# A four-layer graph network on one core: layer 2's scores from stacked high and low parts, layer 3's attention in one bank, centred weights, new orders

## The chip, the cores and the metric

The kernel runs on one core of a Trainium2 chip. Its time is the device time of one execution in microseconds; where several runs are given, their median. Four compute engines work side by side: TensorE (PE in the profile, with its weight loads as PEld), VectorE (DVE), ScalarE (ACT) and GpSimd (POOL); SyncE (SP) issues the DMAs.

## The reference, cut to what matters

128 graphs of 64 nodes with 256 features pass through four layers, each added to its input and normalised over the features.

```python
x = _layernorm(x + _L0_gnn_ref(x, adj, ...), axis=-1)      # hypergraph convolution, twice
x = _layernorm(x + _L1_gnn_ref(x, adj, nodemask, ...), axis=-1)
x = _layernorm(x + _L2_gnn_ref(x, adj, adj, ...), axis=-1)
x = _layernorm(x + _L3_gnn_ref(x, adj, ...), axis=-1)
# layer 2: 8 heads of 32
scores = jnp.einsum('bhqd,bhkd->bhqk', q, k) * SCALE * mask      # mask = adj + adj
ctx = jnp.einsum('bhqk,bhkd->bhqd', jax.nn.softmax(scores, axis=-1), v)
# layer 3
gate = jax.nn.sigmoid(deg * Wd[:, 0] + bd); xg = x * gate
QK = jax.nn.sigmoid(xg @ Wqk.T + bqk)
scores = jnp.einsum('bnd,bmd->bnm', QK, QK) / math.sqrt(D) * adj
attn = scores / (jnp.sum(scores, axis=-1, keepdims=True) + 1e-06)
out = jax.nn.relu(jnp.einsum('bnm,bmd->bnd', attn, xg) @ Wl.T + bl + xg @ Wr.T)
```

## The kernel before

**Tiles and numbers.** A group is four graphs, that is two tiles of 128 rows, each of two graphs (b = 0, 1). There are 32 groups. Every product is taken with operands split into a high and a low part of 16 bits, and three matmuls stand for one (high by high, high by low, low by high; `mm3`, L479 to L483). The splits are made by ScalarE (high part, a cast) and VectorE or GpSimd (low part, a subtraction).

**Steps and streams.** The work of a group is cut into six streams, `stream0` to `stream5` on each engine, which lie in six successive steps: in step s, stream k works on group s - k. Layer 0 is in streams 0 and 1, layer 1 in streams 1 and 2, layer 2 in streams 2 to 4, layer 3 in streams 4 and 5. So 32 + 5 steps are run; those from 6 on are a loop over pairs of steps, the first six and the last five are written out.

**Orders.** On each engine a list written out by hand or by a planner (`ORDER_PE`, `ORDER_ACT`, `ORDER_DVE`, `ORDER_POOL`; `HEAD_...` and `TAIL_...` for the steps outside the loop) tells which stream's next piece comes next. An engine takes its pieces strictly in this order and waits at each for its semaphores.

**SyncE** has one queue in a fixed order (`step`, L436): `place_k` (L386), the loads of the next groups for conv, residual, layer 2, gate and layer 3, those of layer 1, `place_v`, then `store`. Each of them waits on SyncE where it has to, and all behind it waits too.

**Layer 2 scores.** Queries `qh`, `ql` and keys `kst` have the features of four heads on 128 rows. `place_k` copies the keys to a block-diagonal `Kbd` with four copies, zeros elsewhere, so that one matmul of 256 columns gives four heads; 12 such matmuls make the scores of a tile (L677).

**Layer 3 attention** (stream 5) lives in bank bG: projections, sigmoid through tanh, scores of a whole tile of two graphs (128 x 128, masked by a block-diagonal adjacency `atG`), the product with Wr (`o2`, with the bias `blb` added by VectorE, L1237), row sums by matmul (L749), then the mix scaled by the reciprocal of the sums on VectorE (L1252), ReLU on ScalarE (L937), and the residual added on GpSimd (`preG`, L1399).

**Normalisations** B, C, F and G: VectorE's statistics (`stats`, L1021), GpSimd's `rstd` (L1285: add epsilon, power -0.5, two products `nb`), ScalarE's `norm` (L780).

Of the kernel before, what the change touches and what calls it, by code (L numbers as in the profile page):

```python
# [50 lines left out]
HEAD_DVE = [[0, 0, 0, 0, 0, 0, 0, 0, 0, 0, 6, 6, 6, 0, 6, 6, 6, 0, 6, 0, 6, 0, 0], [0, 0, 0, 0, 0, 0, 1, 0, 0, 0, 0, 1, 1, 1, 0, 6, 1, 1, 0, 6, 1, 0, 1, 0, 0], [0, 0, 0, 2, 0, 2, 0, 0, 1, 2, 0, 0, 0, 2, 0, 1, 1, 1, 0, 2, 2, 2, 6, 1, 6, 0, 2, 1, 2, 0, 1, 0, 0, 1], [0, 0, 6, 6, 0, 0, 1, 2, 0, 2, 0, 0, 0, 0, 3, 6, 1, 2, 0, 2, 1, 1, 6, 0, 2, 2, 2, 3, 3, 6, 3, 3, 3, 1, 2, 0, 1, 3, 2, 1, 0, 3, 0, 0, 1, 6], [4, 0, 0, 0, 0, 0, 2, 0, 2, 4, 1, 0, 0, 0, 4, 4, 4, 0, 2, 3, 4, 0, 2, 1, 1, 3, 1, 4, 2, 2, 2, 4, 4, 3, 3, 3, 1, 0, 3, 2, 1, 3, 1, 2, 0, 4, 0, 1, 3, 0], [0, 0, 2, 0, 4, 4, 2, 0, 3, 0, 0, 1, 0, 4, 4, 0, 0, 3, 4, 2, 2, 0, 1, 3, 1, 3, 4, 1, 0, 2, 2, 5, 2, 5, 4, 4, 3, 4, 5, 3, 1, 5, 0, 5, 2, 1, 5, 5, 1, 3, 5, 0, 5, 1, 3, 0, 0, 2, 4]]
HEAD_POOL = [[6, 6, 0, 0, 0, 0, 0, 0, 0, 0, 0, 0], [0, 0, 0, 1, 1, 0, 6, 1, 1, 1, 6, 1, 6, 6, 0, 0, 0, 0, 0, 0], [0, 0, 0, 1, 1, 0, 1, 1, 1, 6, 2, 2, 6, 2, 0, 6, 0, 0, 1, 0, 0, 0], [0, 1, 0, 0, 1, 0, 1, 1, 1, 3, 2, 2, 2, 3, 3, 0, 0, 0, 1, 0, 0, 0], [0, 0, 0, 0, 1, 4, 1, 3, 1, 1, 1, 1, 2, 2, 4, 2, 4, 4, 0, 3, 0, 3, 4, 0, 0, 0, 0], [3, 0, 0, 0, 1, 1, 4, 0, 1, 3, 1, 1, 2, 2, 2, 0, 4, 3, 5, 4, 0, 4, 0, 1, 5, 4, 5, 5, 5, 0, 0, 0]]
TAIL_PE = [[1, 2, 3, 5, 4, 2, 4, 2, 1, 4, 5, 2, 3, 5, 4, 5, 1, 3, 5, 5, 3, 1, 2, 2, 4, 1, 3, 3], [5, 3, 2, 4, 5, 2, 4, 3, 2, 5, 4, 2, 3, 4, 5, 3, 5, 5, 2, 2, 3, 3, 4], [3, 5, 4, 4, 5, 3, 5, 4, 3, 5, 4, 5, 3, 5, 3, 3, 4], [4, 4, 5, 4, 5, 4, 5, 5, 5, 5, 4], [5, 5, 5, 5, 5, 5]]
TAIL_ACT = [[1, 3, 2, 4, 5, 5, 4, 5, 3, 5, 1, 1, 4, 4, 2, 5, 4, 2, 3, 1, 4, 3, 2, 5, 3], [5, 3, 5, 5, 2, 4, 3, 4, 4, 5, 4, 2, 3, 2, 5, 4, 3, 2, 4, 3, 5], [3, 5, 5, 4, 5, 3, 4, 5, 4, 4, 3, 5, 4, 3, 3, 4, 5], [4, 5, 4, 5, 4, 5, 4, 5, 4, 5, 4, 5], [5, 5, 5, 5, 5, 5]]
# [1387 lines left out]
```

## Time and profile before

| | us |
|---|---|
| runs | 997.31, 999.5, 1002.46; median 999.5 |
| the profiled execution | 999.49, of which the span is 997.7 |
| busy of the span: PE, DVE, POOL, ACT | 928.4, 836.6, 746.0, 702.5 |
| mean granted clock of TensorE | 0.977 of full speed |

The span is from the first to the last instruction of the trace. Busy time of an engine is the sum of its instructions' time without overlap. In an order of time ("timeline") each line has the start, the duration of one piece, the engine, the line of the kernel, what is written and what is read, and how many; brackets at the end hold the idle time ahead of it and what ended it. Matmuls overlap, so the cost of a string of them is read from start to start, not from their durations.

### The profile page before, as it was taken

What the parts mean: (1) busy time and instruction counts of PE and PEld (TensorE: products, weight loads), DVE (VectorE), ACT (ScalarE), POOL (GpSimd) and SP (SyncE); (2) the same over time, 40 slices, a digit from 0 to 9 for tenths busy, and PEclk for the clock granted to TensorE, in tenths of its full rate; (3) what the DMA queues carried; (4) which work ended last, traced back from release to release, by engine and by line L of the source; (5) the groups of instructions that cost most, each with busy time, mean ns of one, the idle gap of its engine ahead of it and who ended that gap; (6) DMA issues with size and microseconds to landing.
All of it is one profiled execution on the core that took longest, in us unless ns stands there. A gap on an engine that the chain in (4) does not pass through costs nothing. (4 is left out here: it accounts for less than half of the span.)

```text
span 997.7 us, 32479 instructions
## 1 busy us (share of the span) xinstructions
PE 928.4 (93%) x11228; PEld 812.0 (81%) x11228; DVE 836.6 (84%) x2503; ACT 702.5 (70%) x1516; POOL 746.0 (75%) x1169
## 2 busy tenths in 40 slices
PE   4687899999999999999999999999999999999854
PEld 3566788888888888888888888888888888887642
DVE  4467888898998999899988899899989898988752
ACT  3445667777777777877787777787787777776552
POOL 2655768878878888888888888888888888876551
PEclk9779999999999999999999999999999999999995
DMA  7102221222222222222222222222222222212200
GB/s 238 40 9 60 58 68 50 56 54 61 71 71 71 56 68 53 58 61 61 71 71 71 59 66 56 56 59 65 68 71 71 63 63 67 54 37 52 52 20 21
DMA packets 110231, 61.80 MB, mean 62 GB/s; under 512 B 57072, under 2 KB 105840, under 8 KB 110192
## 3 DMA queue, kind: packets, MB, share of 16 engines
q1 hardware_dynamic: 110192, 61.30, 23.4%
q8 instruction: 22, 0.36, 0.1%
q14 instruction: 17, 0.14, 0.0%
HBM read 35.83 MB, written 8.39 MB: 44 GB/s over the span
## 5 line engine op out<-in xcount | busy, mean ns | idle before, releaser
L784 ACT ACTIVATE late<-preG,nbG,rsG 128x256 f32<-128x256 f32 x64 | 34.9, 592 | 63.1 <-POOL nbG L1295 63.1
L481 PE MATMUL bank<-z1h,W 128*128 128x256 f16 x256 | 72.0, 281 | 3.8 <-DVE z1l L951 3.6
L482 PE MATMUL bank<-z1l,W 128*128 128x256 f16 x256 | 72.0, 281 | 0.0
L483 PE MATMUL bank<-z1h,W 128*128 128x256 f16 x256 | 72.0, 281 | 0.0
L1374 POOL TENSOR_TENSOR late<-late,Smx 128x512 f32<-128x512 f32 x64 | 67.5, 1055 | 4.7 <-DVE Smx L1182 4.7
L481 PE MATMUL bank<-W,rFh 128*128 128x256 f16 x256 | 70.7, 276 | 0.0
L483 PE MATMUL bank<-W,rFl 128*128 128x256 f16 x256 | 70.7, 276 | 0.0
L482 PE MATMUL bank<-W,rFh 128*128 128x256 f16 x256 | 70.7, 276 | 0.0
L1300 POOL TENSOR_TENSOR gp<-late,bdb 128x512 f32<-128x512 f32 x32 | 40.7, 1271 | 32.7 <-ACT late L897 32.7
L813 ACT ACTIVATE r<-bank,b1c 128x256 f32<-128x256 f32 x128 | 52.6, 463 | 16.7 <-PE bank L483 16.7
L1283 POOL TENSOR_TENSOR y0l<-y,y0h 128x512 f16<-128x512 f32 x32 | 37.2, 1163 | 31.6 <-ACT y0h L766 31.6
L1325 POOL TENSOR_TENSOR rsq<-rsq 128x512 f32<-128x512 f32 x32 | 54.6, 1705 | 4.3 <-ACT rsq L821 2.2
L766 ACT ACTIVATE z1h<-bank 128x512 f16<-128x512 f32 x32 | 19.1, 598 | 50.2 <-PE bank L483 50.2
L1283 POOL TENSOR_TENSOR rFl<-r,rFh 128x512 f16<-128x512 f32 x32 | 37.3, 1165 | 18.9 <-ACT rFh L766 18.9
L784 ACT ACTIVATE x<-preB,nbB,rsB 128x256 f32<-128x256 f32 x64 | 34.9, 593 | 22.0 <-POOL nbB L1295 22.0
L677 PE MATMUL bank<-Kbd,qh 128*64 128x256 f16 x512 | 47.1, 279 | 1.9 <-DMA Kbd<-kst 1.7
L951 DVE SCALAR_TENSOR_TENSOR PTl<-bank,PTh 128x512 f16<-128x512 f32 x64 | 43.6, 681 | 2.6 <-ACT PTh L766 2.6
L1399 POOL TENSOR_TENSOR preG<-o3r,late 128x512 f32<-128x512 f32 x32 | 40.8, 1274 | 6.4 <-ACT o3r L937 5.6
L1177 DVE TENSOR_TENSOR late<-bank,acD 128x512 f32<-128x512 f32 x64 | 43.5, 680 | 2.2 <-PE bank L677 2.1
L481 PE MATMUL bank<-Wv,x2Fh 128*128 128x128 f16 x256 | 44.8, 220 | 0.0
L483 PE MATMUL bank<-Wv,x2Fl 128*128 128x128 f16 x256 | 44.5, 219 | 0.0
L482 PE MATMUL bank<-Wv,x2Fh 128*128 128x128 f16 x256 | 44.5, 219 | 0.0
(286 smaller groups left out, 4519.0 us busy)
## 6 DMA issues: line engine op xcount, KB each, us to landing
Vbd<-vst SPq DMA_DIRECT2D x128, 66.0 KB, 2.1
xin<-x SPq DMA_DIRECT2D x32, 256.0 KB, 2.7
xres<-x SPq DMA_DIRECT2D x32, 256.0 KB, 2.9
Kbd<-kst SPq DMA_DIRECT2D x128, 64.0 KB, 2.0
out<-late SPq DMA_DIRECT2D x32, 256.0 KB, 2.2
mrow<-mask SPq DMA_DIRECT2D x32, 128.0 KB, 3.1
atA<-adj_t SPq DMA_DIRECT2D x64, 32.0 KB, 2.3
aC<-adj SPq DMA_DIRECT2D x64, 32.0 KB, 2.1
```

Source lines behind the costliest of these rows:

```text
L481: pe.matmul(o, sh, mh, start=start, stop=False, skip_group_check=True)
L482: pe.matmul(o, sh, ml, start=False, stop=False, skip_group_check=True)
L483: return pe.matmul(o, sl, mh, start=False, stop=stop, skip_group_check=True)
L677: m = pe.matmul(o[64 * b:64 * b + 64, c * 256:(c + 1) * 256], qq[:, c, tok], Kbd[:, :, hl, c, tok], start=(i == 0), stop=(i == 2), skip_gr ...
L784: m = act.activation(dst[:, t], pre[k][:, t], ACT.Identity, bias=nb[k][:, t:t + 1], scale=rs[k][:, t:t + 1])
L813: m = act.activation(r[:, 2 * i + c], (bA, bB)[i][:, c * TOK:(c + 1) * TOK], ACT.Relu, bias=b1c[:, 2 * i + c:2 * i + c + 1], scale=1.0 / WS)
L951: return dve.scalar_tensor_tensor(out=dst, in0=src, scalar=scale, in1=hi, op0=ALU.mult, op1=ALU.subtract)
L1177: dve.tensor_tensor(Sm[:, t], (bD0, bD1)[t][:].rearrange("p (h k) -> p h k", h=HEADS), acD[:, at.par, t:t + 1].broadcast_to([P, HEADS, NOD ...
L1283: return pool.tensor_tensor(dst, a, b, ALU.subtract)
L1325: pool.tensor_tensor(rsq[:, 0:2], rsq[:, 0:2], rsq[:, 2:4], ALU.add).then_inc(ev("sq_sum"), 1)
L1374: pool.tensor_tensor(Ssb[:, t], Sm[:, t], Smx[:, t:t + 1].rearrange("p t h -> p h t").broadcast_to([P, HEADS, NODES]), ALU.subtract).then_ ...
L1399: pool.tensor_tensor(pre["G"][:], o3r[:], x3[:, at.par], ALU.add).then_inc(ev("preG"), 1)
```

## The change

It has five parts.

1. Layer 2's scores. Queries are kept as `qst` with both parts, like `kst`. Both are written to DRAM (`park_q`, `park_k`), and read back by head: 32 rows for a head, with three stacks of 32 rows, `Qs` with high, high, low and `Ks` with high, low, high. One matmul over 96 rows then makes the three products of a head, 64 columns at a time; 16 make a tile's scores. `Kbd` and its clearing go. In SyncE's queue `park_k` takes the first place, `fetch_k` comes behind the loads for conv and residual, `load_layer3` goes behind `place_v`, then `park_q`, `store`, `fetch_q`.
2. Layer 3's attention. Scores are made for each graph alone, 64 x 64 in half of a bank, and masked with their row sums in one operation. They are divided by the sums before the mix (`SAs`, on GpSimd), turned once on TensorE, and split. The bias enters by a matmul of 512 columns, the product with Wr and the mix are added onto it in bG, and VectorE applies ReLU and residual in one operation.
3. Wv1, Wo and bo are centred over the features at the start, so that C and F need no mean: their `rstd` has two operations, and `norm` only a scale. Factors go into the epsilon operations.
4. The second half of `rFl` goes from VectorE to GpSimd; `rsc` comes straight from the power.
5. All orders are new.

```diff
-ORDER_PE = [3, 2, 1, 5, 0, 2, 4, 4, 3, 2, 5, 1, 0, 2, 0, 4, 3, 5, 0, 0, 3, 1, 5, 4, 5, 1, 3, 2, 5, 3, 1, 0, 2, 0, 4]
+ORDER_PE = [1, 2, 3, 5, 3, 0, 4, 4, 2, 1, 2, 0, 5, 4, 0, 2, 5, 3, 3, 0, 1, 0, 4, 5, 1, 2, 5, 3, 5, 2, 3, 1, 0, 0, 4]
-ORDER_ACT = [0, 5, 2, 3, 5, 1, 3, 0, 4, 5, 0, 0, 4, 4, 1, 4, 0, 5, 0, 0, 1, 0, 0, 2, 0, 3, 1, 3, 2, 5, 4, 3, 2, 4, 5]
+ORDER_ACT = [3, 1, 5, 5, 0, 2, 0, 4, 0, 3, 5, 4, 0, 4, 4, 1, 1, 0, 0, 0, 2, 5, 3, 0, 0, 2, 0, 1, 3, 4, 3, 2, 4, 5]
-ORDER_DVE = [0, 2, 0, 0, 2, 0, 0, 0, 0, 4, 1, 3, 4, 0, 4, 0, 2, 4, 4, 2, 5, 1, 0, 1, 3, 1, 5, 0, 2, 2, 2, 5, 3, 4, 3, 3, 3, 1, 5, 4, 0, 4, 5, 4, 5, 1, 5, 2, 1, 0, 3, 0, 5, 5, 1, 0, 3, 2, 4]
+ORDER_DVE = [0, 0, 0, 1, 0, 2, 0, 2, 0, 4, 3, 0, 4, 0, 0, 4, 4, 4, 1, 2, 5, 0, 1, 2, 3, 1, 5, 0, 4, 2, 5, 2, 5, 3, 2, 3, 5, 1, 3, 4, 3, 5, 4, 4, 2, 1, 5, 1, 5, 3, 0, 5, 0, 2, 0, 3, 1, 4]
...
+            def park(name, dram, at):
+
+                sp.dma_start(dram[at.par].rearrange("l p k -> p l k"),
+                             (qst if name == "q" else kst)[:].rearrange("p l c k -> p l (c k)")
+                             ).then_inc(ev(name + "_parked"), 16)
+
+            def fetch(name, dram, dst, parts, at):
+
+                sp.wait_ge(ev(name + "_parked"), at.chain(16, 16)).then_inc(ev("sp_held"), 1)
+                for r, hl in enumerate(parts):
+                    sp.dma_start(dst[32 * r:32 * r + 32].rearrange("p a c k -> p a (c k)"),
+                                 dram[at.par][hl].rearrange("(a p) k -> p a k", p=32)
+                                 ).then_inc(ev(name + "_stacked"), 16)
+
+            def park_q(at):
+                sp.wait_ge(ev("q_lo"), at.n()).then_inc(ev("sp_held"), 1)
+                park("q", q_by_head, at)
+
+            def fetch_q(at):
+                fetch("q", q_by_head, Qs[:, at.par], (0, 0, 1), at)
+
+            def park_k(at):
                 sp.wait_ge(ev("k_lo"), at.n()).then_inc(ev("sp_held"), 1)
+                park("k", k_by_head, at)
+
+            def fetch_k(at):
                 if at.earlier(1):
                     sp.wait_ge(ev("scores"), at.tile(1, -1)).then_inc(ev("sp_held"), 1)
-                for h in range(4):
-                    sp.dma_start(Kbd[32 * h:32 * h + 32, h], kst[32 * h:32 * h + 32]
-                                 ).then_inc(ev(f"k_bd{at.par}"), 16)
+                fetch("k", k_by_head, Ks, (0, 1, 0), at)
...
-                    place_k(at)
-
+                    park_k(at)
                 for k, load in enumerate(loads):
                     at = At(k, j, s + 1)
-                    if load and there(at):
+                    if load and k != 5 and there(at):
                         load(at)
+                    at = At(3, j, s)
+                    if k == 1 and there(at):
+                        fetch_k(at)
...
+                at = At(5, j, s + 1)
+                if there(at):
+                    load_layer3(at)
+                at = At(2, j, s)
+                if there(at):
+                    park_q(at)
                 at = At(5, j, s)
                 if there(at):
                     store(at)
+                at = At(2, j, s)
+                if there(at):
+                    fetch_q(at)
...
-                pe.wait_ge(ev(f"k_bd{at.par}"), at.dma(4))
+                pe.wait_ge(ev("q_stacked"), at.chain(48, 48))
+                pe.wait_ge(ev("k_stacked"), at.chain(48, 48))
...
-                        for i, (qq, hl) in enumerate(((qh, 0), (qh, 1), (ql, 0))):
+                        for a in range(4):
                             for b in range(2):
                                 tok = slice(t * P + 64 * b, t * P + 64 * b + 64)
-                                m = pe.matmul(o[64 * b:64 * b + 64, c * 256:(c + 1) * 256], qq[:, c, tok],
-                                              Kbd[:, :, hl, c, tok], start=(i == 0), stop=(i == 2),
+                                h = 4 * c + a
+                                m = pe.matmul(o[64 * b:64 * b + 64, h * NODES:(h + 1) * NODES],
+                                              Qs[:, at.par, a, c, tok], Ks[:, a, c, tok], start=True, stop=True,
                                               skip_group_check=True)
...
+                pe.wait_ge(ev("attn_scaled"), at.n())
+                pe.transpose(bG[:, D + P:2 * D], SAs[:].rearrange("p b k -> p (b k)"), ident[:]
+                             ).then_inc(ev("attn_turned"), 1)
...
+                pe.matmul(bG[:].rearrange("p (t d) -> p t d", t=TILES), ones16[:, 0:1].broadcast_to([P, P]),
+                          blr[:].rearrange("p (o d) -> p o d", o=1).broadcast_to([P, TILES, D]), start=True, stop=False,
+                          skip_group_check=True)
+                for t in range(TILES):
+                    m = project_tm(bG[:, t * D:(t + 1) * D], xgFh, xgFl, Wr, t, onto=True)
                 m.then_inc(ev("o2_raw"), 1)
...
+                    for i, (sa, y) in enumerate(((SAh, y3h), (SAh, y3l), (SAl, y3h))):
+                        for b in range(2):
+                            rows = slice(64 * b, 64 * b + 64)
+                            m = pe.matmul(bG[rows, t * D:(t + 1) * D], sa[rows, t], y[rows, t], start=False,
+                                          stop=(i == 2), skip_group_check=True)
                 m.then_inc(ev("o1"), 1)
...
+                for b in range(2):
+                    m = dve.tensor_tensor_reduce(SA[:, b], bG[:, D + b * NODES:D + (b + 1) * NODES], atG[:, at.par, b],
+                                                 1.0, 0.0, ALU.mult, ALU.add, bG[:, b:b + 1])
+                m.then_inc(ev("attn"), 1)
...
+                dve.scalar_tensor_tensor(out=pre["G"][:].rearrange("p t k -> p (t k)"), in0=bG[:], scalar=0.0,
+                                         in1=x3[:, at.par].rearrange("p t k -> p (t k)"), op0=ALU.max, op1=ALU.add
+                                         ).then_inc(ev("preG"), 1)
...
-                dve.wait_ge(ev("rF_hi"), at.tile(1))
-                dve.tensor_tensor(rFl[:, 2:4], r[:, 2:4], rFh[:, 2:4], ALU.subtract).then_inc(ev("rF_lo1"), 1)
-                yield
...
+                pool.wait_ge(ev("rF_hi"), at.tile(1))
+                sub(rFl[:, 2:4], r[:, 2:4], rFh[:, 2:4]).then_inc(ev("rF_lo1"), 1)
+                yield
...
-                pool.wait_ge(ev("attn_hi"), at.n())
-                sub(SAl[:].rearrange("p t k -> p (t k)"), SA[:], SAh[:].rearrange("p t k -> p (t k)")
-                    ).then_inc(ev("attn_lo"), 1)
-                yield
-                pool.wait_ge(ev("o3_relu"), at.n())
-                if at.earlier(1):
-                    pool.wait_ge(ev("xG"), at.n(-1))
-                pool.tensor_tensor(pre["G"][:], o3r[:], x3[:, at.par], ALU.add).then_inc(ev("preG"), 1)
+                pool.wait_ge(ev("row_scale"), at.chain(2, 2))
+                pool.tensor_tensor(SAs[:], SA[:], srec[:].rearrange("p (t o) -> p t o", o=1).broadcast_to(
+                    [P, TILES, NODES]), ALU.mult).then_inc(ev("attn_scaled"), 1)
```

## Rows read from the trace of the kernel before

**Rows 1.** The page, part 1: busy us, share of the span, instructions of each engine.

```profile
PE 928.4 (93%) x11228; PEld 812.0 (81%) x11228; DVE 836.6 (84%) x2503; ACT 702.5 (70%) x1516; POOL 746.0 (75%) x1169
```

**Rows 2.** Windows, one step: length, busy PE, PEld, DVE, ACT, POOL; clock, DMA share, GB/s.

```profile
525.33:553.18 27.85, 27.85 (x352) 25.02 (x350) 25.21 (x78) 21.63 (x47) 22.96 (x36) 1.00 0.24 64
```

**Rows 3.** Timeline of SyncE: start us, duration us, what, count.

```profile
194.74 2.49 SPq L392 DMA_DIRECT2D Kbd<-kst  x4
...
529.34 0.42 SPq L407 DMA_DIRECT2D out<-late  x1
...
532.34 2.48 SPq L392 DMA_DIRECT2D Kbd<-kst  x4
...
535.09 0.40 SPq L345 DMA_DIRECT2D xin<-x  x1
...
538.30 0.37 SPq L369 DMA_DIRECT2D acD<-adj  x1
...
840.07 2.48 SPq L392 DMA_DIRECT2D Kbd<-kst  x4
```

**Rows 4.** Timeline of TensorE, one step: start us, duration us, what, count.

```profile
524.84 0.66 PE L506 MATMUL bank<-ident,late 128*128 128x128 f32 x4
...
525.33 0.27 PE L481 MATMUL bank<-x2Fh,Wk 128*128 128x256 f16 x1
...
529.91 0.26 PE L701 MATMUL bank<-Vbd,PTh 128*64 128x66 f16 x4
...
530.80 0.23 PE L481 MATMUL bank<-Wv,x2Fh 128*128 128x128 f16 x1
...
537.04 0.41 PE L677 MATMUL bank<-Kbd,qh 128*64 128x256 f16 x4
...
537.82 0.23 PE L481 MATMUL bank<-Qh 128*128 128x128 f16 x1
...
538.50 0.27 PE L481 MATMUL bank<-z1h,W 128*128 128x256 f16 x1
...
547.39 0.27 PE L481 MATMUL bank<-y3h,SAh 128*128 128x256 f16 x1
...
548.04 0.60 PE L688 MATMUL bank<-ident,E 128*128 128x128 f32 x4
...
553.18 0.27 PE L481 MATMUL bank<-x2Fh,Wk 128*128 128x256 f16 x1
```

**Rows 5.** Timelines of ScalarE and VectorE, the beginning of the same step.

```profile
525.53 0.60 ACT L766 ACTIVATE xgFh<-bank 128x512 f16<-128x512 f32 x1 [0.98 <-PE bank L506]
...
526.18 0.68 DVE L951 SCALAR_TENSOR_TENSOR xgFl<-bank,xgFh 128x512 f16<-128x512 f32 x1
...
526.77 0.32 DVE L1035 TENSOR_SCALAR HT<-atA 128x256 f16<-128x256 f32 x1
...
529.87 0.16 DVE L1060 TENSOR_SCALAR Dbg<-bank 128x2 f32<-128x2 f32 x1 [0.72 <-PE bank L557]
...
531.24 0.88 DVE L957 SCALAR_TENSOR_TENSOR kst<-bank,bkc,kst 128x256 f16<-128x256 f32 x2 [0.23 <-ACT kst L869]
```

**Rows 6.** Instruction groups by form: busy us, mean ns, idle before.

```profile
L1237 DVE SCALAR_TENSOR_TENSOR late<-bank,blb 128x512 f32<-128x512 f32 x32 | 21.8, 680 | 3.6 <-PE bank L483 3.6
...
L1295 POOL TENSOR_SCALAR nbF<-mvF,rsF 128x1 f32<-128x1 f32 x64 | 16.0, 267 | 6.2 <-POOL rsF L1291 6.0
...
L1399 POOL TENSOR_TENSOR preG<-o3r,late 128x512 f32<-128x512 f32 x32 | 40.8, 1274 | 6.4 <-ACT o3r L937 5.6
```

**Rows 7.** Chain of work that ended last, tail: start us, us, what.

```profile
941.94 2.05 DMA Kbd<-kst
944.03 0.85 PE bank L677 x12
```

**Rows 8.** DMA issues: KB each, median us from issue to landing.

```profile
out<-late SPq DMA_DIRECT2D x32, 256.0 KB, 2.2
...
acD<-adj SPq DMA_DIRECT2D x32, 64.0 KB, 2.4
```

More of the change, by code:

```diff
@@ L129, in build @@
         x3, x4 = [v.rearrange("p a (t d) -> p a t d", t=TILES) for v in (x3, x4)]
-        cx, gw, xg, o2, o3 = [late[1][:, i] for i in range(5)]
+        cx, gw, xg = [late[1][:, i] for i in range(3)]
         Sm, Ssb = [v.rearrange("p t (h k) -> p t h k", h=HEADS) for v in (Sm, Ssb)]
@@ L864, in stream3 @@
             def stream3(at):
+                if at.earlier(1):
+                    act.wait_ge(ev("k_parked"), at.chain(16, 16, -1))
                 act.wait_ge(ev("k"), at.n())
-                if at.earlier(1):
-                    act.wait_ge(ev(f"k_bd{1 - at.par}"), at.before().dma(4))
                 for c in range(2):
@@ L977, in part, with centre @@
                     low(W[:, 1], split_from[name], W[:, 0], WS).then_inc(ev("unstaged"), 1)
+                def centre(rows, sums, done):
+                    dve.tensor_reduce(wmean[:, sums], rows, AX.X, ALU.add).then_inc(ev("centring"), 1)
+                    dve.wait_ge(ev("centring"), done + 1)
+                    dve.tensor_scalar(wmean[:, sums], wmean[:, sums], -1.0 / D, None, ALU.mult
+                                      ).then_inc(ev("centring"), 1)
+                    dve.wait_ge(ev("centring"), done + 2)
+                    for i in range(rows.shape[1]):
+                        k = sums.start + i
+                        m = dve.tensor_scalar(rows[:, i], rows[:, i], wmean[:, k:k + 1], None, ALU.add)
+                    m.then_inc(ev("centring"), 1)
                 dve.wait_ge(ev("w2_in"), 64)
@@ L1009, in set_up @@
                 m.then_inc(ev("setup"), 1)
+                dve.tensor_scalar(blr[:], blf[:], WS, None, ALU.mult).then_inc(ev("bl_row"), 1)
+                dve.wait_ge(ev("bl_row"), 1)
+                low(blr[32:33], blf[32:33], blr[32:33], WS).then_inc(ev("bl_row"), 1)
                 yield
-                for i in range(2, 7):
+                part(2)
+                yield
+                dve.wait_ge(ev("second_in"), 32)
+                centre(stages["Wv1"], slice(0, 2), 0)
+                yield
+                part(3)
+                yield
+                dve.wait_ge(ev("rest_in"), arrival("Wo")[1])
+                centre(stages["Wo"], slice(2, 4), 3)
+                yield
+                centre(bob[:].rearrange("p (o d) -> p o d", o=1), slice(4, 5), 6)
+                yield
+                for i in range(4, 7):
                     part(i)
@@ L1246, in stream5 @@
                 yield
[L1247 to L1254 removed]
+                dve.wait_ge(ev("attn_hi"), at.n())
@@ L1270, in set_up @@
             def set_up():
-                for h in range(4):
-                    pool.memset(Kbd[:, h], 0.0).then_inc(ev("ident"), 1)
-                    yield
                 for par in range(2):
```

199 lines of the change are left out of this document (99 added, 100 removed).

## The prediction

> **What bounds the kernel now.** I read the page's busy line first: TensorE is busy 93% of the span, VectorE 84% [rows 1]. The window of one whole step in the middle shows more: TensorE busy all of its 27.85 us, VectorE 25.2, at the full granted clock [rows 2]. Then SyncE's order of time: the first copy of layer 2's keys is issued at 194.74 and at 840.07, 23 steps apart, so a step costs 28.06 us on average [rows 3]; 26 steps run like that, and the first six and last five are partly filled. TensorE's own order of time gives the places inside a step, which I count from the end of the turn of `xg` (525.33, the last item of `ORDER_PE`, in both orders): scores of tile 0 at 11.71, next step at 27.85 [rows 4]. Nothing but TensorE's work sets the time in these steps. Last, what lies ahead of the scores on other engines: ScalarE and VectorE take `xgF` first, then a string of short operations, then the low half of `kst` [rows 5], then SyncE's four issues [rows 3].
>
> **The change, part by part.** All of it per step, in us.
>
> TensorE. (a) Scores: the two tiles took 12 matmuls of 256 columns each, 0.78 a tile (537.04 to 537.82). Now 16 matmuls of 64 columns a tile. The nearest row is the context product, 48 matmuls of 66 columns in 0.89 (529.91 to 530.80), 0.0185 each [rows 4]: 0.30, or 0.37 with the entry into the pattern. Two tiles save 0.82. (b) Layer 3 scores: 0.68 (537.82 to 538.50) becomes 24 matmuls of 64 columns, 0.44: saves 0.24. (c) One more turn of 128 columns: a quarter of 0.49 (524.84 to 525.33), 0.12; the bias row, 512 columns at twice 0.108 (six of 256 columns in 0.65, 547.39 to 548.04), 0.22. (d) `o1`, six matmuls of 256 columns over 128 rows, becomes twelve over 64 rows. If the two halves of a pair run beside each other, as the 64-column pairs of the context product do, it stays 0.65, plus 0.08 for leaving the pattern; if they follow one another it is 1.30. I take the first. Row sums and their waits are counted at nothing. Sum: -0.82 -0.24 +0.12 +0.22 +0.08 = -0.64, between -0.9 and 0.0. TensorE alone would make the step 27.4.
>
> VectorE loses `o2` (0.68) and half of `rFl`, and gains a 128-column low part; GpSimd loses `preG` (1.27) and the two `nb` of C and of F (0.27 each), and gains `rFl`'s other half; ScalarE loses the ReLU [rows 6]. None of these ends a step today [rows 2], so this is worth nothing in the 26 steps.
>
> SyncE and DMA. Four copies of keys go; a write of K to DRAM, a wait, three reads, and the same for Q come: eight for four. Q has a whole step. K has not, and this is the part that I cost in full.
> - VectorE's step begins 1.44 after the turn of `xg`, since `xgFh` and `xgFl` come first (525.33 to 526.77 [rows 5]); the new orders end with the same three items.
> - From there to the low part of `kst` it was 4.47, of which 0.72 was a wait for TensorE and 0.23 a wait for ScalarE [rows 5]. The new order has the same operations ahead of it but one of 0.08: 3.44. The keys are now projected third on TensorE, done by 2.8, and ScalarE's part is over by 3.8 if it is as long as VectorE's; no wait. So it starts at 4.9 and ends at 5.77 (0.88 long). SyncE issues 0.22 later, as now (532.12 to 532.34 [rows 3]): 5.97.
> - `park_k` takes one issue, 0.42 with 0.27 behind it, as a store does [rows 3]. Then, in the same queue and ahead of `fetch_k`, come the loads of x, of two blocks of the adjacency and of the residual: 3.21 (535.09 to 538.30 [rows 3]). The write lands in 2.2, like the store [rows 8], so within that time. `fetch_k` starts at 5.97+0.69+3.21+0.1 = 9.97.
> - Its third issue starts 1.24 later (0.62 each, 2.48 for four [rows 3]) and lands in 2.05 (copy within SBUF [rows 7]) to 2.4 (load [rows 8]); I take 2.2, nearest to a store or load of this size. Keys are there at 13.4, between 12.9 and 14.2 (the ends: three issues at 0.5 and the short landing; issues at 0.8, as the blocks with short rows take, and the long one).
> - TensorE's items ahead of scores are the same set as before plus layer 3's scores, 11.71+0.44 = 12.15. It waits 1.25.
> - Behind the wait lies all of its queue: what took 16.14 (537.04 to 553.18) less 0.68, 0.82 and plus 0.42 is 15.06. A step is 13.4+15.06 = 28.46, against 28.06: +0.40, between 0 and +1.2. Over 26 steps +10.
>
> The Trainium skill (DMA: Bandwidth & Descriptors, "Anatomy of one DMA") says that most of a transfer's fixed 2 us is the receipt of its write, heaviest where the target is HBM. The rows here show 2.2 for the store to DRAM and 2.05 within SBUF, so the heavier target costs 0.2; by either figure the write is covered by the loads queued behind it.
>
> Why the wait isn't repaid: VectorE's start is tied to TensorE's last item, so what TensorE waits moves the next chain by as much.
>
> Edges. In the last steps no loads stand between, so K costs 0.4+2.2+1.2+2.2 = 6.0 from the low part where now it is 1.9+2.05 = 3.95 [rows 3, 7]: +2 at each of two to three places. The chain through layer 3 loses a GpSimd addition (1.27), `o2` (0.68), and 0.54 for each pair of `nb` of C and F [rows 6], and the ReLU, some of it in two places: about -6 in the last steps. The head loses GpSimd's clearing of `Kbd`, which nothing waits for, and gains centring on VectorE. I put 0 on the edges, between -5 and +6. Profiled execution 999.49 (span 997.7), the median 999.5: the same. Sum: 1010.
>
> **Rivals.** One: the keys arrive in time and TensorE stays dense. For it: the copies now have 0.8 in hand (issued at 7.01 after the origin, landed by about 10.9, used at 11.71), and an error of 1.2 in a chain of ten terms is possible. Then a step is 27.4, 26 times -0.66 is -17, with the shorter layer 3 chain -3: 979. Against it: the ready time would have to be 12.15, and even the short ends of all DMA terms give 12.9.
>
> Two: `o1`'s halves follow one another. The row at issue is 547.39, six matmuls that use all 128 rows; no row shows a 64-row one. 0.65 more per step, behind the scores and so on the path: +17, that is 1027; slower from the point where the pair overlaps by less than nine tenths. The Trainium skill (TensorEngine Tiling (Array Packing), "Gotcha 1: PSUM Pressure" and "Key Properties") states that row tiles can't use one PSUM bank at the same time and that a change of tiling mode drains the engine, and both halves of `o1` write the bank bG. No row here shows it; by this rule the sum would be this rival's.
>
> Three: SyncE is late at `park_k`. Ahead of it stand the store and `fetch_q`: the store was issued at 529.34, 4.0 after the origin [rows 3]; GpSimd's string for G is a bit shorter and earlier, so I take 3.1, an estimate, then 0.7 and three issues of 0.62: free at 5.7, 0.3 before it is needed. If the stacked reads take 0.8 an issue, this slips by 0.3 and `fetch_k` by 0.4, and with a store as late as today by 0.9 more: about +1 a step, 1036.
>
> That the change doesn't do what it says (K no longer on the path at all) is rival one.
>
> **How the numbers follow.** Forecast 1010 (own range 1000 to 1022), chance 0.46; rival one 979, 0.26; two 1027, 0.14; three 1036, 0.14. The range leaves out one in ten on each side: 977 to 1035. Half a per cent, 5 us, is about what a measurement of this kernel can tell from no change. Faster by more (under 994.5): rival one and a little of the forecast, 0.28. Within: a quarter of the forecast and the slow edge of rival one, 0.16. Slower: 0.56. Step by step the weakest term is the landing of 128 KB reads with 32 rows each, which the trace of before doesn't hold.
>
> **What would show it.** TensorE's line idle once per step ahead of the first score matmul, about 1.2 us, released by a DMA into `Ks`; the rest of the step dense; a step of 28.4 between issues; score tiles of 0.37 apart; `o1` in 0.65 to 0.73; VectorE's share lower. The issues from `park_k` to the first `fetch_k` 4 us apart. If scores start within 0.1 of the item ahead, the chain was mis-sized and rival one holds; if the idle time is released by Q's reads, it is rival three; a second idle place in the step would be one that I have not costed.

## The result, and the profile after

The changed kernel takes 1083.3 us (median of 4 runs, 1079.0 to 1088.6); the kernel before, beside it, 998.4 us. The ratio is 1.085, with a 95% interval of 1.078 to 1.093: slower by 85 us, where the prediction had 1010. The profiled execution has a span of 1086.7 us.

The page of the changed kernel: busy time of each engine, the clock line of the 40 slices, two lines of the parts on the chain and on DMA issues, and the group of layer 2's scores.

```profile
PE 949.9 (87%) x11996; PEld 825.9 (76%) x11996; DVE 792.9 (73%) x2548; ACT 676.9 (62%) x1484; POOL 686.0 (63%) x1005
...
PEclk9798899989999999899999999998999999999997
...
PE 42%; DVE 15%; SPq 13%; DMA 11%; issue 10%; POOL 4%; ACT 4%; POOLq 0%; ACTq 0%; DVEq 0%
...
L719 PE MATMUL bank<-Ks,Qs 96*64 96x64 f16 x1024 | 29.3, 219 | 72.4 <-DMA Ks<-k_by_head 72.2
...
Ks<-k_by_head SPq DMA_DIRECT2D x96, 128.0 KB, 3.0
```

Every engine but TensorE is busy for less time than before [rows 1], so no engine became the bound. TensorE's busy time *rose* by 21.5 us though it has less to do, and its share fell from 93% to 87%. Two things have to be explained: the idle time, of which 72.2 us stand ahead of layer 2's scores and are released by the reads into `Ks`, and the busy time, which is a matter of the granted clock. Its mean is 0.930, where it was 0.977. In the clock line a 9 stands for 90% or more, so only the 8s show that something is new in the middle of the kernel; the line of the kernel before has none there:

```profile
PEclk9779999999999999999999999999999999999995
```

SyncE and DMA hold 24% of the chain.

One step of the changed kernel, from the end of the turn of `xg` (516.96) to the next (547.86), cut at the scores. Columns as in [rows 2].

```profile
516.96:547.86 30.90, 28.76 (x376) 25.47 (x375) 23.83 (x80) 20.82 (x46) 21.35 (x32) 0.94 0.32 92
...
516.96:531.48 14.52, 12.38 (x194) 11.21 (x193) 14.29 (x50) 11.00 (x24) 11.27 (x19) 1.00 0.52 159
531.48:536.84 5.36, 5.36 (x60) 4.39 (x61) 2.08 (x6) 1.23 (x3) 2.42 (x5) 0.68 0.38 86
536.84:547.86 11.02, 11.02 (x124) 9.86 (x122) 7.45 (x25) 8.59 (x20) 7.65 (x9) 1.00 0.02 5
```

Ahead of the scores TensorE is idle for 2.14 us (14.52 less 12.38). Behind them it is never idle, but for 5.4 us it works at a granted clock of 0.68; then the clock is full again. TensorE's timeline shows where in that stretch:

```profile
531.48 0.69 PE L719 MATMUL bank<-Ks,Qs 96*64 96x64 f16 x32 [2.14 <-DMA Ks<-k_by_head]
532.11 0.28 PE L520 MATMUL bank<-z1h,W 128*128 128x256 f16 x1
...
532.81 0.42 PE L521 MATMUL bank<-z1l,W 128*128 128x256 f16 x1
...
534.09 0.42 PE L521 MATMUL bank<-z1l,W 128*128 128x256 f16 x1
...
534.52 1.06 PE L545 MATMUL bank<-ident,x 128*128 128x128 f32 x4
...
535.37 0.42 PE L520 MATMUL bank<-z1h,W 128*128 128x256 f16 x1
535.59 0.33 PE L521 MATMUL bank<-z1l,W 128*128 128x256 f16 x1
535.75 0.27 PE L522 MATMUL bank<-z1h,W 128*128 128x256 f16 x1
```

From 532.4 to 535.6 a matmul of 256 columns starts every 0.215 us, before and after every 0.108: the lower of the two levels (1.2 and 2.4 GHz) for 3.2 us, which makes W1's first half 2.41 us instead of 1.32, its second half 1.47, the turn of x1 0.85 instead of 0.44: 1.7 in all.

SyncE's timeline has the chain that the wait is for (start, duration, what), and the same place one step later:

```profile
523.37 0.38 SPq L394 DMA_DIRECT2D k_by_head<-kst  x1
524.01 0.40 SPq L350 DMA_DIRECT2D xin<-x  x1
524.80 1.42 SPq L334 DMA_DIRECT2D atA<-adj_t  x2
526.40 0.46 SPq L359 DMA_DIRECT2D xres<-x  x1
527.12 1.29 SPq L402 DMA_DIRECT2D Ks<-k_by_head  x3
...
551.85 0.41 SPq L434 DMA_DIRECT2D out<-late  x1
552.37 1.38 SPq L402 DMA_DIRECT2D Qs<-q_by_head  x3
554.33 0.38 SPq L394 DMA_DIRECT2D k_by_head<-kst  x1
```

and the chain of waits through it:

```profile
527.50 0.42 SPq L402
527.98 3.37 DMA Ks<-k_by_head
531.48 0.69 PE bank L719 x32
```

K is written at 523.37, 6.4 after the origin. The three reads start 3.75 later, behind the loads of x, of the adjacency and of the residual. Each takes 0.43 to issue, and the third lands after 3.37. That is no outlier: over the 24 full steps the median of the third read, the one that ends the wait, is 3.36; the 3.0 of the page is the median of all 96 reads. From the issue of the write to the landing of the third read the median is 8.19. The mean step, from the first x load in the full steps to the last (177.92 to 896.86, 23 steps), is 31.26 us, where it was 28.06 [rows 3].

### The profile page after: what moved, and what is told of

Same layout as the page of the kernel before. It is cut to its first block, busy times and chain, and to the rows that moved or that the text cites. A ratio compares the mean times of both kernels' runs of the same rounds, so it can differ in the third digit from the quotient of the medians.

```text
span 1086.7 us, 33947 instructions
## 1 busy us (share of the span) xinstructions
PE 949.9 (87%) x11996; PEld 825.9 (76%) x11996; DVE 792.9 (73%) x2548; ACT 676.9 (62%) x1484; POOL 686.0 (63%) x1005
## 4 chain that ended last, share of the span: by engine, by line
PE 42%; DVE 15%; SPq 13%; DMA 11%; issue 10%; POOL 4%; ACT 4%; POOLq 0%; ACTq 0%; DVEq 0%
PE bank L520 11%; DMA Ks<-k_by_head 10%; PE bank L521 10%; PE bank L522 10%; SPq L402 5%; SPq L334 4%; PE bank L545 3%; PE bank L719 2%; PE bank L730 2%; PE bank L805 2%; DVE stG L1106 2%; SPq L350 1%; SPq L359 1%; DVE wscr L1197 1%; DVE kst L1010 1%
## 5 line engine op out<-in xcount | busy, mean ns | idle before, releaser
L1358 POOL TENSOR_TENSOR rFl<-r,rFh 128x512 f16<-128x512 f32 x64 | 74.3, 1163 | 103.0 <-ACT rFh L816 101.6
L816 ACT ACTIVATE x1Fh<-bank 128x512 f16<-128x512 f32 x32 | 19.1, 596 | 132.9 <-PE bank L545 132.9
L719 PE MATMUL bank<-Ks,Qs 96*64 96x64 f16 x1024 | 29.3, 219 | 72.4 <-DMA Ks<-k_by_head 72.2
L520 PE MATMUL bank<-z1h,W 128*128 128x256 f16 x256 | 87.1, 340 | 5.0 <-DVE z1l L1004 5.0
L522 PE MATMUL bank<-z1h,W 128*128 128x256 f16 x256 | 86.2, 337 | 0.0
L719 PEld LDWEIGHTS bank<-Ks,Qs 96*64 96x64 f16 x1024 | 25.6, 133 | 76.7 <-issue 76.5
L1004 DVE SCALAR_TENSOR_TENSOR x1Fl<-bank,x1Fh 128x512 f16<-128x512 f32 x32 | 22.1, 690 | 75.4 <-ACT x1Fh L816 75.4
L869 ACT ACTIVATE r<-bank,b1c 128x256 f32<-128x256 f32 x128 | 53.3, 471 | 16.6 <-PE bank L522 16.4
L545 PE MATMUL bank<-ident,x 128*128 128x128 f32 x256 | 45.4, 307 | 4.4 <-ACT x L838 3.5
L838 ACT ACTIVATE late<-preF,rsF 128x256 f32<-128x256 f32 x64 | 29.0, 501 | 31.7 <-POOL rsF L1369 31.7
L1468 POOL TENSOR_TENSOR late<-g,late 128x512 f32<-128x512 f32 x32 | 40.8, 1275 | 12.2 <-ACT late L838 12.2
L1358 POOL TENSOR_TENSOR xl<-xin,xh 128x512 f16<-128x512 f32 x32 | 37.6, 1174 | 17.2 <-ACT xh L816 17.2
```

Source lines behind the costliest of these rows:

```text
L520: pe.matmul(o, sh, mh, start=start, stop=False, skip_group_check=True)
L522: return pe.matmul(o, sl, mh, start=False, stop=stop, skip_group_check=True)
L545: m = pe.transpose(o[:, c * TOK + t * P:c * TOK + (t + 1) * P], src[:, t, c * P:(c + 1) * P], ident_[:])
L719: m = pe.matmul(o[64 * b:64 * b + 64, h * NODES:(h + 1) * NODES], Qs[:, at.par, a, c, tok], Ks[:, a, c, tok], start=True, stop=True, skip_ ...
L869: m = act.activation(r[:, 2 * i + c], (bA, bB)[i][:, c * TOK:(c + 1) * TOK], ACT.Relu, bias=b1c[:, 2 * i + c:2 * i + c + 1], scale=1.0 / WS)
L1358: return pool.tensor_tensor(dst, a, b, ALU.subtract)
```

## Experiments

The steps below are means over the full steps, counted like that. The prediction's account of the wait (the place of `fetch_k` in SyncE's queue makes the keys late, and TensorE waits) is the theory at the start. Its rivals: some other part of the change costs the time (layer 3, `o1` on half arrays, the orders), or the wait costs more than its length.

### Without the detour through DRAM

The changed kernel, with the scores of the kernel before: keys copied within SBUF to `Kbd`, issued where `park_k` stood. All else is changed as in the diff.

```diff
+            def place_k(at):
                 sp.wait_ge(ev("k_lo"), at.n()).then_inc(ev("sp_held"), 1)
...
+                for h in range(4):
+                    sp.dma_start(Kbd[32 * h:32 * h + 32, h], kst[32 * h:32 * h + 32]
+                                 ).then_inc(ev(f"k_bd{at.par}"), 16)
...
-                    at = At(3, j, s)
-                    if k == 1 and there(at):
-                        fetch_k(at)
```

> The changed kernel with one part undone: layer 2's scores again from the block-diagonal keys in SBUF (12 matmuls of 256 columns a tile, four copies, no DRAM), the rest and the new orders kept. Theory (the DRAM detour is the whole loss): no wait ahead of the scores, TensorE at full clock, step 30.9 - 2.14 (wait) - 1.5 (half clock) + 0.8 (wider scores) = 28.1, total 1083 - 26 * 2.8 = 1010 less 5 to 10 at the edges: 1000 to 1010. Rival (the new orders or layer 3's new form hold something up as well): a second idle place, 1030 or more.

Measured: 988.6 us, 0.985 of before (0.982 to 0.988), a step of 27.69. All of the loss, 95 us, hangs on the stacked scores and their DMAs; the rest of the change is a *gain* of some 14 us, more than was expected of it. The windows of 100 us in the middle of three kernels (changed, this one, and the next) show the difference:

```profile
500.00:600.00 100.00, 92.23 (x1191) 81.50 (x1192) 74.32 (x243) 64.51 (x144) 66.52 (x98) 0.93 0.33 90
```

```profile
500.00:600.00 100.00, 100.00 (x1345) 90.25 (x1343) 86.26 (x285) 76.74 (x171) 76.28 (x111) 1.00 0.28 71
```

```profile
500.00:600.00 100.00, 99.98 (x1363) 90.06 (x1361) 86.32 (x284) 75.54 (x167) 79.31 (x119) 1.00 0.36 100
```

### The same DMAs, in another place of the queue

`fetch_k` moved up: the reads follow the write at once, and the loads come after.

```diff
                     park_k(at)
+                    fetch_k(at)
                 for k, load in enumerate(loads):
...
-                    at = At(3, j, s)
-                    if k == 1 and there(at):
-                        fetch_k(at)
```

> Same work; SyncE issues the three reads of the stacked keys right behind the write, ahead of the loads of x, adjacency and residual. Theory (queue order): reads start 2.6 after the write's issue and not 3.8, and with no large load ahead of them they land in 2.3 to 2.7 and not 3.4; keys ready 6.0 to 6.4 after the issue where it was 8.1, at 12.4 to 12.8 of the step; TensorE waits 0.1 to 0.6, keeps its clock: step 27.4 to 27.9, total 990 to 1005. Rival (a read of DRAM rows written just before takes 3 us or more wherever it stands): ready at 13.1 to 13.5, wait about 1 and part of the half clock: 1020 to 1045.

Measured: 975.0 us, 0.971 (0.967 to 0.975), a step of 27.12, 15 us under the range. Two lines moved take 108 us off the changed kernel. SyncE's timeline has the reads 2.5 behind the write where it was 3.75, and the loads behind them:

```profile
521.96 0.38 SPq L394 DMA_DIRECT2D k_by_head<-kst  x1
...
524.48 1.25 SPq L402 DMA_DIRECT2D Ks<-k_by_head  x3
...
526.00 0.40 SPq L350 DMA_DIRECT2D xin<-x  x1
```

The wait on the write, in which SyncE does nothing, has no cost that shows. And the reads land sooner. The first line is of the changed kernel, the second of this one:

```profile
DMA to landing us min/median/max: 2.3/3.0/4.9
```

```profile
DMA to landing us min/median/max: 2.1/2.5/3.7
```

These are all three reads of a step together; the third alone goes from a median of 3.36 to 2.57. From the issue of the write to the last landing it is 5.89 where it was 8.19: 1.5 by the order, 0.8 by the landing. And the clock stays at 1.00.

### What the low clock costs

Work that nobody needs, ahead of the stacked waits, to see whether the low clock comes from TensorE's standing still. First 18 matmuls of 256 columns in float16:

```diff
                 yield
+                pe.wait_ge(ev("k_lo"), at.n())
+                for _ in range(18):
+                    pe.matmul(bD0[:, 0:D], W1[:, 0, 0, 0:P], W1[:, 1, 0, 0:D], start=True, stop=True,
+                              skip_group_check=True)
                 pe.wait_ge(ev("q_stacked"), at.chain(48, 48))
```

> Same work plus 18 matmuls of 256 columns (1.95 us) on constant operands into a free bank just ahead of the wait for the stacked parts, in every step; their result is overwritten. Nothing that anyone waits for comes sooner. Theory (the wait of 2.1 us makes the chip halve TensorE's clock, which costs 1.5 a step): granted clock 1.00 in the loop, step 29.4, total 1043 to 1050. Rival (the half clock has another cause, or the fill costs as much as it saves): 1080 or more.

Measured: 1135.1 us, 1.131 (1.128 to 1.134), far outside. The waits of TensorE in this kernel (what it waited for: total, times, longest) show a new one, and the page's queue of instructions what goes with it:

```profile
PE bank L521 <- issue: 33.9, 12, 3.2
PE bank L520 <- issue: 31.1, 12, 2.8
...
PE bank L723 <- DMA Ks<-k_by_head: 10.3, 14, 1.6
```

```profile
q8 instruction: 133, 2.18, 0.8%
```

The changed kernel fetches instructions in 24 packets (0.39 MB), this one in 133 (2.18 MB). From 240 to 980 us, inside the loop, the changed kernel has none and this one 100, and twice in each turn of the loop (two steps) TensorE stands for 2.7 us with nothing to wait for. The wait for the keys is nearly gone, but the run mixes two effects, and the low clock isn't gone, though the next expectation says so: 0.97 is granted in the middle 100 us, and the low stretches now lie behind these new pauses. The second form does the same with two matmuls of 512 columns in float32, four instructions a step:

```diff
+                pe.wait_ge(ev("k_lo"), at.n())
+                for _ in range(2):
+                    pe.matmul(bD0[:], onesf[:], betb[:].rearrange("p c k -> p (c k)"), start=True, stop=True,
+                              skip_group_check=True)
```

> As filler, but the time ahead of the wait is filled by two matmuls of 512 columns on 32-bit constants (4 instruction rows a step for 18, about 1.75 us). Theory: in filler the half clock was gone, and what it lost instead was idle time of 2.5 to 3 us twice per pair of steps in which TensorE's instructions were fetched again (133 packets of instructions for 24); with few instructions that doesn't come, and the clock's share of the loss shows: granted clock 0.99 or more in the loop, instruction packets about 24, step 29.4 to 29.9, total 1040 to 1055. Rival: the idle stretches come from the extra wait or the extra work itself and stay: 1100 or more. Second rival: clock stays at 0.93: 1083.

Measured: 1033.9 us, 1.030 (1.023 to 1.037), a little under the range; a step of 29.30, instruction packets back at 24. The same 100 us:

```profile
500.00:600.00 100.00, 99.56 (x1265) 85.29 (x1266) 80.55 (x261) 71.17 (x157) 73.30 (x107) 1.00 0.34 93
```

The kernel does *more* work than the changed one, its keys land nearly as late (median of all reads 2.9; from the write's issue 7.97 for 8.19), and it is 49 us faster: the clock is 1.00 in all full steps. So the low clock of the changed kernel comes from TensorE's idle time ahead of the scores. It costs 2.0 us a step by this run, of which 0.2 may be the sooner keys, and 1.9 by the changed kernel's granted clock, 0.94 over its full steps.

### Scores later on TensorE

The other way to hide the keys: scores moved behind W1's second half and the turn of x1 in `ORDER_PE`, `ORDER_DVE` fitted to it, no DMA moved.

```diff
-ORDER_PE = [1, 2, 3, 5, 3, 0, 4, 4, 2, 1, 2, 0, 5, 4, 0, 2, 5, 3, 3, 0, 1, 0, 4, 5, 1, 2, 5, 3, 5, 2, 3, 1, 0, 0, 4]
+ORDER_PE = [1, 2, 3, 5, 3, 0, 4, 4, 2, 1, 2, 0, 5, 4, 0, 2, 5, 0, 1, 0, 3, 3, 4, 5, 1, 2, 5, 3, 5, 2, 3, 1, 0, 0, 4]
```

> Same work; in the loop's order of TensorE both score tiles stand behind the first projection's second half (z of layer 0) and the turn of x1, 3.2 us of other work later, and VectorE's order is moved to fit. Theory (only the distance between the keys' projection and the scores is short): keys at 14.5, TensorE at the scores at 15.4, no wait, clock 1.00, step 27.3 to 27.8, total 985 to 1000. Rival (the wait moves to the next user: softmax, context, or VectorE behind the scores): another idle place of 1 or more, 1010 or more.

Measured: 1000.4 us, 0.998 (0.996 to 1.000), at the upper edge; a step of 27.77, as expected, with no wait for keys in the full steps but one of 0.6 in the first, and the clock at 1.00. It is still 0.65 a step behind the kernel with the reads moved. TensorE's items in one step show small gaps that count as busy: W1's halves 1.62 and 1.41 (1.32 and 1.31 in the kernel with both moves, below), the turn between them 0.49 (0.43), the one behind `Gm` 0.58 (0.44), `u` 0.84 (0.67). What had stood behind the scores now stands sooner; that it runs there at the heels of VectorE is my reading of it, and no run shows it. And the few steps at the start and the end, whose orders I left, keep the wait (six times, with that one):

```profile
PE bank L719 <- DMA Ks<-k_by_head: 12.4, 6, 3.8
```

### The parts of the late keys

Whether the landing is long because of the loads queued ahead of the reads: the loads of x (for the convolution and for the residual), 256 KB each, cut to 32 of their 256 columns from the third group on. This kernel leaves the rest of x out and computes with stale values.

```diff
-                sp.dma_start(xin[:, at.par], at_group(xv, at)).then_inc(ev(f"x_in{at.par}"), 16)
+                n = 32 if at.earlier(2) else D
+                sp.dma_start(xin[:, at.par, :, 0:n], at_group(xv, at)[:, :, 0:n]).then_inc(ev(f"x_in{at.par}"), 16)
```

> The changed kernel, same number of DMAs in the same order, but the two loads of x (for conv and residual) bring 32 of the 256 columns from group 2 on, so x is stale in the rest and the output is not the reference's. Theory (the reads of the keys land late, 3.4 and not 2.2, because 512 KB of loads were issued in the 4 us before them and share the 16 DMA engines): the last read lands in 2.2 to 2.6, keys ready 0.8 to 1.2 earlier, step 29.9 or, if the clock is kept as well, 28.4; total 1005 to 1060. Rival (a read over 32 rows takes 3 us by itself): 1075 to 1085, landing 3.0 as now.

Measured: 1031.2 us, 1.028 (1.021 to 1.035), a step of 29.19: inside the range. The landing of all reads falls from 3.0 to 2.6 at the median, that of the third from 3.36 to 2.62, with the order of issues as it was:

```profile
DMA to landing us min/median/max: 2.2/2.6/3.8
```

52 us for 0.74 us of landing a step (about 19 us over 26 steps): the total wait falls from 72.2 to 50.1, which is 22, and the rest is about what the clock gives back, which holds for most of the time with the shorter waits (0.98 in the same 100 us, 0.93 in the changed kernel).

Whether SyncE comes late to `park_k` (rival three of the prediction): `fetch_q` put ahead of the store of the output.

```diff
                     park_q(at)
-                at = At(5, j, s)
-                if there(at):
-                    store(at)
                 at = At(2, j, s)
...
                     fetch_q(at)
+                at = At(5, j, s)
+                if there(at):
+                    store(at)
```

> Same work; the three reads of the stacked queries stand ahead of the store and not behind it, so the keys' write is never held back by ScalarE's last norm. Theory (SyncE late at the keys' write is only 0.1 to 0.3 us in half of the steps): total 1074 to 1083. Rival three of the prediction (the held write is a large part): 1060 or less.

Measured: 1072.1 us, 1.068 (1.060 to 1.075), a step of 30.71: 0.55 a step better, just beyond the expected edge. Rival three is there, and it is a small part.

### The stacked scores alone

The kernel before with the stacked scores and their DMAs alone, as the diff places them, and the orders of before: if the new orders or layer 3 were needed for the loss, it would be absent here.

```diff
+            def park_k(at):
...
+                    park_k(at)
...
+                    at = At(3, j, s)
+                    if k == 1 and there(at):
+                        fetch_k(at)
...
+                                m = pe.matmul(o[64 * b:64 * b + 64, h * NODES:(h + 1) * NODES],
+                                              Qs[:, at.par, a, c, tok], Ks[:, a, c, tok], start=True, stop=True,
```

> The kernel before with the first part of the change alone: stacked scores through DRAM, with the old orders, old layer 3, no centring. Theory (the chain from the keys' low part is 8.1 us whatever the orders): write issued at 7.0 of the step, keys ready at 15.1, TensorE at the scores at 11.7: wait 3.4, half clock after it 1.7, narrower scores -0.8: step 32.4, total 1105 to 1115. Rival (the new orders brought part of the loss): 1060 or less.

Measured: 1129.7 us, 1.123 (1.116 to 1.131). The step is the expected 32.4, the total 15 us over the range, in the steps outside the full ones. The waits have all of it in one line:

```profile
PE bank L711 <- DMA Ks<-k_by_head: 100.9, 32, 5.7
```

So the loss needs only part one of the change. The rest of it wins back some 46 us here and 14 in the run without the detour; the sizes differ because here it also shortens the wait (100.9 to 72.2 in all).

This run has something else to tell. Of its 24 full steps, all with waits of 3.0 to 3.6, five weren't followed by the low clock. One of them, the wait and the granted clock of the 9 us behind it:

```profile
412.91 0.44 PE L711 MATMUL bank<-Ks,Qs 96*64 96x64 f16 x16 [3.19 <-DMA Ks<-k_by_head]
```

```profile
412.91:422.00 9.09, 9.09 (x114) 7.89 (x115) 6.51 (x12) 6.51 (x15) 6.00 (x9) 1.00 0.27 59
```

So a wait longer than nearly all of those that cost the changed kernel its clock can pass without loss. The length of the wait isn't all that decides; what else does, no run here was made to show.

The same kernel with `fetch_k` right behind `park_k`:

> The kernel before with the stacked scores alone, old orders, the keys' reads issued right behind their write. Theory (chain of 6.2 to 6.5 us from the write's issue at 7.0): keys ready at 13.2 to 13.5 of the step, TensorE at the scores at 11.7, wait 1.5 to 1.8, clock kept in most steps as in small_loads: step 28.06 - 0.8 + 1.7 = 28.9 to 29.4, total 1020 to 1045. Rival (the new orders aren't needed, the queue order is all): no wait, step 27.3, total 980.

Measured: 1028.0 us, 1.024 (1.021 to 1.027), in the range, and a step of 28.56, a little under it: 102 us for the move here, 108 there. What is left of the wait from 300 to 800 us is short:

```profile
PE bank L709 <- DMA Ks<-k_by_head: 12.6, 17, 1.1
```

So with the old orders the stacked scores lose 2.4% even in the good place of the queue; with the new ones they win. Of the 30 us that the profiled span is longer than before, 13 are in the full steps (28.56 for 28.06), where a wait of 0.6 to 1.2 is left (once 1.8), and 17 in the first and last steps, where waits of up to 5.5 stand. Which part of the new orders takes them away was not run.

### A version ahead of both

Both moves of SyncE's queue together (the two diffs above).

> Same work; both moves on SyncE together: the reads of the keys right behind their write, and the reads of the queries ahead of the store. Theory (TensorE is dense at 27.1 a step once the keys' reads go first; the second move takes away the last few tenths of waiting and something in the first and last steps): total 966 to 975, step 26.9 to 27.1. Rival (the moves are worth the same half a microsecond each time, as q_first against the changed kernel): step 26.6, total 962 or less.

Measured: 971.7 us, 0.970 (0.967 to 0.972), a step of 26.96, as expected; 3% faster than before, 10% faster than the changed kernel.

```profile
500.00:600.00 100.00, 100.00 (x1379) 90.54 (x1378) 87.14 (x289) 76.92 (x172) 79.21 (x115) 1.00 0.35 102
```

TensorE is dense again, and its work alone ends a step.

## Why the prediction was wrong in size

Right were the direction, the place and the mechanism of the wait: one idle stretch per step, ahead of the first score matmul, released by a read into `Ks`, the rest dense. The size, +10, was an eighth of what came, +85, and the range ended at 1035. By its own terms, each counted from the turn of `xg`:

| term | predicted | measured in the step shown |
|---|---|---|
| low part of `kst` ends | 5.77 | 6.3 |
| SyncE issues the write | 5.97 | 6.4 (one step later 6.5) |
| write's issue to the next | 0.69 | 0.64 |
| loads ahead of the reads | 3.21 | 3.11 (3.5 in every second step) |
| third read starts after the first | 1.24 | 0.86 |
| third read lands in | 2.2 (2.05 to 2.4) | 3.37 (median of the third reads 3.36) |
| keys there | 13.4 | 14.4 (scores start at 14.5) |
| TensorE at the scores | 12.15 | 12.4 |
| its wait | 1.25 | 2.14 |
| behind the wait | 15.06 | 16.4 |
| step | 28.46 | 30.90 (mean 31.26) |

**The landing** was the worst of the mis-sized terms, and I had called it the weakest. I took it from transfers that stood alone in their queue: the store and the copy in [rows 7, 8]. Here the reads stand behind two 256 KB loads and two blocks of the adjacency; the DMA share is 0.52 in the first 14.52 us of the step. For the third read, 3.36 with the loads, 2.62 with small ones and 2.57 with the loads behind (three runs) give this term: +1.2 a step, of which some 0.8 is the loads and 0.4 the read itself. The bound "2.05 to 2.4" was made of rows with other neighbours; the row [rows 8] for `acD` was the only one with a transfer behind large ones, and it has half the size.

The write's landing, put at 2.2, is 2.5 at the median, and the loads cover it, as forecast. The section of the Trainium skill that the prediction names for it (DMA: Bandwidth & Descriptors, "Anatomy of one DMA") describes transfers that GpSimd issues; these are SyncE's, and the rows decide.

**VectorE's string** ended 0.5 later. `xgFl` starts 1.15 after the turn instead of 0.85, since `PTl` (0.68) stands right ahead of it. The other 0.2 is in the string: the two operations of `HBh` take 0.95 where they took 0.41. **SyncE** was, in the second step shown, held by the store (issued at 4.0 after the turn, as before; I had estimated 3.1) and by `fetch_q`, so that the write came right behind: what rival three said, at half its price, in part of the steps (q_first, 0.55 a step).

**The clock was missing altogether.** The sum priced a wait at its length. A wait of 2.14 us was followed by 3.2 us at the lower level, +1.7 in the step shown. This is the step that failed, more than any number. The prediction read the granted clock of 1.00 in [rows 2] as a given, but that was read from a step in which TensorE never stood still. filler32 shows it (−2.0 a step for filling the wait), small_loads shows how steep it is: 0.74 us less of landing a step, and 52 us came back. By the steps of small_loads, none of 13 waits between 1.2 and 1.6 us was followed by the low clock, and 5 of 11 between 1.66 and 2.03 were; in q_first one of 1.74 was not, and all 23 from 1.75 to 2.32 were. The two kernels are 41 us apart, for half a us of wait a step. But that is a count in these two kernels and no rule: in stack_only five waits of 3.19 to 3.55 were not followed by it.

**The step closes**: keys 1.1 later than forecast, and behind the wait +1.7 of clock less 0.4 for cheaper items; 2.4 together on 28.46 is 30.9. The mean of all steps, 31.26, holds four of 32.4 to 33.5. It closes by itself as well: 26.96 of work (both_first), a mean wait of 2.5 and 1.9 of clock are 31.4. 3.2 a step over 26 steps is +83 of the 89 between the two profiled spans, so the edges were worth +6, at the end of the range given for them.

Two sums of the prediction are off by themselves, and too little to matter here. It built its step of 28.46 on one of 27.85 and held it against the mean of 28.06; against 27.85 it is +0.61 a step and +16, not +10. And the ends of its ready time come out of its own terms as 13.0 and 14.0, not 12.9 and 14.2.

**TensorE's terms** held, mostly on the cheap side. Score tiles 0.31 each (0.37), layer 3's scores 0.41 (0.44), turn 0.11 (0.12), bias row 0.22 (0.22). `o1` is settled by its timeline:

```profile
542.07 0.30 PE L805 MATMUL bank<-y3h,SAh 64*64 64x256 f16 x2
...
542.64 0.27 PE L805 MATMUL bank<-y3h,SAl 64*64 64x256 f16 x2
...
542.84 0.28 PE L520 MATMUL bank<-x2Fh,Wq 128*128 128x256 f16 x1
```

Twelve matmuls in 0.77, where the serial case had 1.30: the halves of a pair share their time, in one bank. Rival two is refuted, and so is, for this pair, the rule of the Trainium skill (TensorEngine Tiling (Array Packing), "Gotcha 1: PSUM Pressure") that row tiles can't use a PSUM bank at the same time; here the two write different halves of its partitions. Where page and timeline differ, the timeline decides. TensorE alone was put at 27.4 a step and measures 26.96 (both_first): the row sums' 0.10, cheaper entries (0.13 of it in the scores, 0.61 for both tiles), and the 0.2 between the mean of 28.06, which I had treated as work, and the step of 27.85 in [rows 2].

**Rival one** described a kernel that the queue could have given. It was rightly held to be unlikely with this queue; with the reads moved it is what happens, at 975 and 972 where it said 979. The reason against it, that even the short ends give 12.9, was sound for that place in the queue, but the prediction asked only whether the reads could be in time *there*, and took the 3.21 of loads ahead of them as cover for the write. What they covered was a wait of SyncE that cost nobody anything.

**The statement of causes.** Shown by runs: the detour's place (fetch_first, stack_only_first), the clock (filler32), the landing (small_loads), SyncE's order (q_first), and that nothing else of the change costs (kbd). They overlap, as each shortens the wait on which the clock hangs, so their sizes don't add up. Why the rest of the change is worth 13.6 us (kbd) is only read from the traces: shorter strings on VectorE, GpSimd and ScalarE and the cheaper items above; its parts weren't run one by one.

## What to carry to other kernels

In a queue in order, put the short transfer that an engine waits for ahead of the prefetches, even if its issuer must stand and wait a little: two lines moved turned +8.5% into −2.9%. Price a wait of the engine that bounds the kernel not at its length but with what its clock does after it, and price a landing by a row with the same neighbours in the queue. And when the wait can't be moved away, a little useless work in few instructions was worth more than idling (−49 us), though no more than half of what the right order gave.

## What the runs showed of the hardware

- After an idle stretch of 2.14 us TensorE ran 0.9 us at full clock and then 3.2 us at half, in a loop that was otherwise dense. Recurring idle stretches of up to 1.6 us (13 steps of small_loads) passed without it, and so did five of 3.19 to 3.55 us in stack_only, where 19 of 3.0 to 3.6 us didn't.
- A loop of TensorE that grew by 36 matmuls in two steps (x12572 instead of x11996 over the run) made the instruction queue fetch 133 packets instead of 24, and the engine stood 2.7 us twice a turn, put down to issue; that the fetching is the cause is read from the two going together. Four instructions more a step (x12124) did not.
- 128 KB reads from DRAM in 32 rows land in 2.5 at the median with nothing large ahead, 3.0 (up to 4.9) behind loads of more than half a megabyte; of three in a row the last suffers most, 2.57 against 3.36. Issuing one takes 0.43, three tenths less than the copies within SBUF (0.62).
- Two matmuls of 64 rows by 64 columns on opposite corners of the array, into the two halves of one bank's partitions, run side by side: 12 in 0.77.
